# Six one-hots from one comparison with a scalar in a graph network kernel

## What is computed

```python
msg_input = jnp.concatenate([node_feats[src], edge_sh, edge_radial], axis=-1)
h = jax.nn.silu(msg_input @ W1 + b1)
h = jax.nn.silu(h @ W2 + b2)
messages = h @ W3 + b3
aggregated = jax.ops.segment_sum(messages, dst, num_segments=node_feats.shape[0])
```

## Time and profile before

| | |
|---|---|
| median of three timed runs | 4085.32 us |
| the profiled execution, its own time | 4067.74 us |
| its span | 4066.0 us |
| mean granted TensorE clock, share of full | 0.839 |
| PE busy (matmuls) | 3010.0 us, 74% |
| DVE busy | 1891.9 us, 47% |
| POOL busy | 1628.2 us, 40% |
| ACT busy | 1567.3 us, 39% |

### The profile page before, as it was taken

The page is one execution under the profiler, slowest core; times in us unless marked ns, Lnnn a source line. Parts: engine busy times, 40 slices in busy tenths (PEclk is TensorE's granted clock), DMA queues, the critical chain, the costliest instruction groups (busy, mean ns, idle before and its releaser), DMA issues.

```text
span 4066.0 us, 65736 instructions
## 1 busy us (share of the span) xinstructions
PE 3010.0 (74%) x21771; PEld 2333.6 (57%) x21771; DVE 1891.9 (47%) x2455; ACT 1567.3 (39%) x2617; POOL 1628.2 (40%) x1563
## 2 busy tenths in 40 slices
PE   3699997799963777776778777666777776677747
PEld 3477776798961455554555555554545555455546
DVE  5999998444550433333333333333334333333405
ACT  2688885233221333332333333333333333333415
POOL 3000000000006566665555666665554666656240
PEclk9999998899985888887878888887778888878866
DMA  2133333698971333333333333333333333333310
GB/s 101 80 156 144 158 144 156 256 366 326 360 248 31 90 89 85 87 86 76 86 84 88 89 86 87 86 84 80 80 79 85 88 86 87 85 80 89 87 22 16
DMA packets 204771, 477.12 MB, mean 117 GB/s; under 512 B 47656, under 2 KB 99034, under 8 KB 185709
## 3 DMA queue, kind: packets, MB, share of 16 engines
q1 hardware_dynamic: 153573, 422.33, 30.6%
q0 software_dynamic: 50144, 52.47, 7.5%
q10 hardware_dynamic: 1001, 1.66, 0.1%
HBM read 339.87 MB, written 136.41 MB: 117 GB/s over the span
## 4 chain that ended last, share of the span: by engine, by line
PE 53%; another core or an unknown queue 24%; issue 9%; DVE 9%; ACT 4%; DMA 1%; POOL 0%; DVEq 0%; ACTq 0%; POOLq 0%
PE ps L795 11%; PE ps L968 8%; PE ps L980 8%; PE ps L987 8%; PE ps L995 7%; PE ps L814 5%; PE ps L958 4%; DVE arena L1903 2%; DVE stageT L1879 1%; ACT ps L1351 1%; ACT arena L1346 1%; PE ps L1067 1%; PE ps L1044 0%; PE ps L846 0%
## 5 line engine op out<-in xcount | busy, mean ns | idle before, releaser
L663 POOL DMA_INDIRECT arena<-m_tab,m_idx x1463 | 1543.8, 1055 | 2207.5 <-issue 1574.7
L2150 DVE TENSOR_TENSOR_SCAN arena<-arena,ps 128x512 f32<-128x512 f32 x391 | 500.0, 1279 | 1294.4 <-ACT ps L1351 985.3
L995 PEld LDWEIGHTS ps<-weights,arena 128*128 128x128 f32 x3128 | 477.3, 219 | 537.8 <-issue 529.6
L995 PE MATMUL ps<-weights,arena 128*128 128x64 f32 x3128 | 468.3, 296 | 296.3 <-issue 229.0
L1346 ACT ACTIVATE arena<-ps,weights 128x512 f32<-128x512 f32 x391 | 268.4, 687 | 864.2 <-remote 390.6
L958 PE MATMUL ps<-ident,arena 128*64 128x128 f32 x1564 | 268.0, 298 | 383.0 <-DVE arena L2137 238.7
L980 PE MATMUL ps<-arena,weights 81*128 81x512 f32 x782 | 477.6, 692 | 71.0 <-issue 38.6
L795 PE MATMUL ps<-arena 128*128 128x195 bf16 (+1 forms) x4802 | 481.9, 248 | 32.2 <-DVE arena L1845 31.6
L968 PE MATMUL ps<-ends,arena 128*128 128x192 bf16 x4900 | 461.7, 250 | 29.3 <-issue 27.0
L987 PE MATMUL ps<-arena,weights 128*128 128x512 f32 x782 | 464.5, 676 | 13.7 <-issue 12.3
L795 PEld LDWEIGHTS ps<-arena 128*128 128x128 f16 x4802 | 417.1, 98 | 63.0 <-DVE arena L1845 31.7
(11 more groups left out here) (277 smaller groups left out, 2365.4 us busy)
## 6 DMA issues: line engine op xcount, KB each, us to landing
arena<-count_d SPq DMA_DIRECT2D x98, 1568.0 KB, 8.5
arena<-keep_d SPq DMA_DIRECT2D x391, 256.0 KB
count_d<-arena SPq DMA_DIRECT2D x49, 1568.0 KB, 5.1
scan_rows<-arena SPq DMA_DIRECT2D x391, 128.0 KB
arena<-m_tab,m_idx POOLq DMA_INDIRECT x1463
arena<-attr_in SPq DMA_DIRECT2D x391, 34.0 KB
arena<-src_row SPq DMA_DIRECT2D x25, 256.0 KB
wide<-hT_d SPq DMA_DIRECT2D x1, 1617.0 KB
```

Source lines behind the costliest of these rows:

```text
L663: pool.indirect_dma_start(m_rows[:, k, t, :], None, m_tab, bass.IndirectOffsetOnAxis(ap=m_idx[:, k, t:t + 1].bitcast(U32), axis=0))\
L995: last = pe.matmul(m_back[k % BACK_RING][:, t * D:(t + 1) * D], m_scan[:, k % SCAN_RING, t * P:(t + 1) * P], W("W3"), start=True, stop=True)
L2150: dve.tensor_tensor_scan(m_scan[:, k % SCAN_RING, :], m_mask[:, k % MASK_RING, :], m_term[k % TERM_RING], before, ALU.mult, ALU.add).then_ ...
```

## The change

The comparison with a table of numbers becomes a comparison with a scalar. At the beginning of a lap the source numbers are laid six times, the copy `a` less 128 a, in int16. Each group of six blocks is then one TENSOR_SCALAR that compares all six copies with one number a partition, `node_no[:, first]` = p + 128 first. The table `pick_no`, the small TENSOR_SCALAR of each group and two waits of each group go. The groups become eight of six blocks and one of one block. A copy has 516 numbers rather than 512, in three runs of 172; the six copies lie in three rows of 1032 numbers with a gap of two behind each, and the loaded numbers in three rows of 172 with a gap of two.

```diff
-PICKS = [(0, 6), (6, 6), (12, 6), (18, 6), (24, 5), (29, 5), (34, 5), (39, 5), (44, 5)]
+PICKS = [(a, min(6, J - a)) for a in range(0, J, 6)]
 PICK_RING, PICK_BLOCKS, PICK_LAG = 3, 6, 5
+PICK_RUNS, PICK_RUN = 3, 172
+PICK_COLS = PICK_RUNS * PICK_RUN
+PICK_PAIR = 2 * PICK_COLS
...
-        pick_int = carve(slots_at, BE).bitcast(I32)
-        pick_src, pick_from = (carve(slots_at + BE + n * BE // 2, BE // 2).bitcast(I16) for n in range(2))
-        pick_no = stage[:, :, :, :].rearrange("p s t f -> p (s t f)")[:, 0:PICK_BLOCKS * BE // 2].bitcast(I16)\
-            .rearrange("p (a e) -> p a e", a=PICK_BLOCKS)
+        pick_int = carve(slots_at, PICK_RUNS * (PICK_RUN + 2)).bitcast(I32)\
+            .rearrange("p (r e) -> p r e", r=PICK_RUNS)[:, :, 0:PICK_RUN]
+        pick_src = stage[:, :, :, :].rearrange("p s t f -> p (s t f)")[:, 0:PICK_BLOCKS // 2 * (PICK_PAIR + 2) // 2].bitcast(I16)\
+            .rearrange("p (r e) -> p r e", r=PICK_BLOCKS // 2)[:, :, 0:PICK_PAIR]
...
             def load_pick(lap):
-                sp.dma_start(pick_int, src_row[:, bass.ds((LOOP * lap + PICKED) * BE, BE)].partition_broadcast(P)).then_inc(pick_loaded, DMA)
+                sp.dma_start(pick_int, src_row[:, bass.ds((LOOP * lap + PICKED) * BE, PICK_COLS)].partition_broadcast(P)
+                             .rearrange("p o (r e) -> p (o r) e", r=PICK_RUNS)).then_inc(pick_loaded, DMA)
...
                 dve.wait_ge(pick_loaded, DMA * lap)
-                dve.tensor_copy(pick_src, pick_int).then_inc(pick_known, 1)
+                dve.wait_ge(pick_ready, len(PICKS) * (lap - 1) + 1)
+                for a in range(PICK_BLOCKS):
+                    last = dve.tensor_scalar(pick_src[:, a // 2, (a % 2) * PICK_COLS:(a % 2 + 1) * PICK_COLS]
+                                             .rearrange("p (r e) -> p r e", r=PICK_RUNS), pick_int, float(-P * a), None, ALU.add)
+                last.then_inc(pick_known, 1)
+                dve.wait_ge(pick_known, lap)
...
             def mark_pick(lap, n):
 
                 first, blocks = PICKS[n]
-                dve.wait_ge(pick_known, (1 + len(PICKS)) * (lap - 1) + n + 1)
-                dve.wait_ge(pick_ready, len(PICKS) * (lap - 1) + n + 1)
-                dve.tensor_scalar(pick_from, pick_src, float(-P * first), None, ALU.add).then_inc(pick_known, 1)
-                dve.wait_ge(pick_known, (1 + len(PICKS)) * (lap - 1) + n + 2)
                 dve.wait_ge(pick_used, len(PICKS) * (lap - 1) + n + 1)
-                dve.tensor_tensor(pick[:, n % PICK_RING, 0:blocks, :], pick_from.unsqueeze(1).to_broadcast([P, blocks, BE]),
-                                  pick_no[:, 0:blocks, :], ALU.is_equal).then_inc(pick_ready, 1)
+                of = pick[:, n % PICK_RING, 0:blocks * PICK_COLS]
+                if blocks == PICK_BLOCKS:
+                    of, src = of.rearrange("p (r e) -> p r e", r=PICK_BLOCKS // 2), pick_src
+                else:
+                    src = pick_src[:, 0, 0:blocks * PICK_COLS]
+                dve.tensor_scalar(of, src, node_no[:, first:first + 1], None, ALU.is_equal).then_inc(pick_ready, 1)
...
-                    link(dve.tensor_copy(pick_no, per_node(node_no[:, 0:PICK_BLOCKS], BE)))
```

More of the change, by code:

```diff
@@ L200, in build @@
         slots_at += OUT_RING * TB * D
-        pick = carve(slots_at, PICK_RING * PICK_BLOCKS * BE // 2).bitcast(BF16).rearrange("p (k a e) -> p k a e", k=PICK_RING, a=PICK_BLOCKS)
-        slots_at += PICK_RING * PICK_BLOCKS * BE // 2
-        pick_int = carve(slots_at, BE).bitcast(I32)
-        pick_src, pick_from = (carve(slots_at + BE + n * BE // 2, BE // 2).bitcast(I16) for n in range(2))
-        pick_no = stage[:, :, :, :].rearrange("p s t f -> p (s t f)")[:, 0:PICK_BLOCKS * BE // 2].bitcast(I16)\
-            .rearrange("p (a e) -> p a e", a=PICK_BLOCKS)
+        pick = carve(slots_at, PICK_RING * PICK_BLOCKS * PICK_COLS // 2).bitcast(BF16)\
+            .rearrange("p (k c) -> p k c", k=PICK_RING)
+        slots_at += PICK_RING * PICK_BLOCKS * PICK_COLS // 2
+        pick_int = carve(slots_at, PICK_RUNS * (PICK_RUN + 2)).bitcast(I32)\
+            .rearrange("p (r e) -> p r e", r=PICK_RUNS)[:, :, 0:PICK_RUN]
+        pick_src = stage[:, :, :, :].rearrange("p s t f -> p (s t f)")[:, 0:PICK_BLOCKS // 2 * (PICK_PAIR + 2) // 2].bitcast(I16)\
+            .rearrange("p (r e) -> p r e", r=PICK_BLOCKS // 2)[:, :, 0:PICK_PAIR]
         node_parts = ends[:, :, :].rearrange("p j f -> p (j f)")[:, 0:J * PARTS * D // 2].bitcast(BF16)\
@@ L569, in _ @@
                     move_slot(LOOP * i + k, k)
-                sp.wait_ge(pick_known, (1 + len(PICKS)) * (i - 1) + 1)
+                sp.wait_ge(pick_known, i)
                 load_pick(i + 1)
@@ L968, in pick_rows @@
                         last = pe.matmul(ps[:, 3 + TERM_RING + t // 2, (t % 2) * PARTS * D:(t % 2 + 1) * PARTS * D],
-                                         pick[:, n % PICK_RING, a - first, t * P:(t + 1) * P],
+                                         pick[:, n % PICK_RING, (a - first) * PICK_COLS + t * P:(a - first) * PICK_COLS + (t + 1) * P],
                                          node_parts[:, a, :, :].rearrange("p q d -> p (q d)"),
```

## The result

| | kernel before | changed kernel |
|---|---|---|
| median, us (4 runs each, one chip) | 4090.5 | 4514.94 |
| from, to | 4084.05, 4100.86 | 4501.55, 4526.65 |
| ratio, 95% interval | | 1.1034 [1.0992, 1.1076] |
| profiled execution, its span | 4067.74, 4066.0 | 4501.55, 4499.8 |

It is 10.3% slower; 4500 was forecast.

What follows compares the result with a forecast made beforehand. It took laps to be bounded by PE's work plus freezes during POOL's unheld gathers: 117.9 us a lap against 100.5, times 24, adds 418 to 4067.7, and with 17.6 gives 4500 us; its own range was 4390 to 4600.

Steps and rivals of the forecast that it cites:

- The compare: Lap stage, DVE: each 3096-element compare takes 1.76 us and does not hold POOL's gathers.
- Rival A: Lap stage: the compare runs short, 0.94 us, and part of the hold on gathers stays; 4265 us, chance 0.12.
- Rival B: Lap stage: the compare takes 1.76 us and holds gathers as the old one does; 4085 to 4111 us, chance 0.10.
- Hidden beside PE: Lap stage: DVE's marks, 14.4 us a lap, stand beside PE's picks and cost nothing.
- The source numbers: Lap start, DVE: six casts take 2.4 to 4.1 us instead of 0.4; 0 to 1.2 us a lap come through.
- The inference on which the prediction hung: Lap stage: the other engines freeze after some 8 us of unheld POOL gathers, and held gathers prevent it.
- The lap of 3003: Kernel before: a lap whose marks held few gathers froze at 26 us and took 112.5 us.
- Rival C: Freeze tied to place in the program or burst length, not unheld gathers; 154 us less, 3931 us, chance 0.15.
- an onset of 10 us: Pick-stage bursts: freeze allowed to begin at 10 us, not 8, as small DVE operations may hold a gather; 117.9 us a lap.
- three bursts of 25, 25 and 20 us: POOL's gathers per lap after the change: the 40 split in two, since the second 20's indices need PE.
- 4.1 us of recovery: Lap stage: time at half clock after each freeze, 4.1 us, for two freezes a lap before and three after.
- A lap = PE's 61.2 + frozen time ...: Lap stage: a lap is PE's 61.2 us, plus frozen time less what PE does in it, plus recovery at half clock.

Runs made afterwards that it cites:

- two_runs: The changed kernel with the source numbers in two spaced runs of 1548 instead of three of 1032: 3275.46 us, 0.9631 of the kernel before.
- tensor_tensor_again: The changed kernel with its eight long compares made by tensor_tensor again, layout, casts and grouping kept: 4133.86 us, 1.0136 of the kernel before.
- fewer_gathers: The changed kernel with 52 instead of 56 gathers a lap, output not the reference's: 3066.35 us, 0.9007 of the kernel before.
- chip 5: The changed kernel run unaltered on a chip where the kernel before took 3406.99 us: 3184.24 us, 0.9347 of it.
- paced form: The changed kernel with GpSimd waiting for the scan ahead of each slot's four gathers but the first of five: 3176.51 us, 0.9354 of the kernel before.
- the pacing of the old kernel: The kernel before with GpSimd waiting for the scan ahead of each slot's four gathers but the first of five: 3983.29 us, beside 4179.38 unaltered.

## Why the prediction was right, and where it was not

*The compare.* 1.80 us against 1.76, and no hold: right. Of the two reasons given, the one read from the rows doesn't stand: "it is cut differently on both sides" is as true of two_runs, two runs against one, which takes 1.017 us and holds. The one on the counts, three against 3096 and neither both even nor equal, agrees with both runs. The 1.76 was the row of another operation; that it came within 0.04 is in part luck. Rival A (short, partial hold) is what two_runs is. Rival B needed the hold to stay; it is gone.

*Hidden beside PE.* Right: leaving the compares out gave 3180 against 3184 us. That was measured where nothing freezes; with the freeze it wasn't tried.

*The source numbers.* 0.678 us a cast, 4.1 a lap, the upper end. What of it came through I can't separate: the table's residue is under 20 us either way.

*The inference on which the prediction hung*, that held gathers prevent the freeze: tensor_tensor_again, on a chip that freezes, shows that the operation which holds them keeps the freeze off; that the holding does it remains an inference. The lap of 3003 was misread: six of its gathers were held, not few, and its freeze began during one. "8 us after the last held gather" fits the usual laps and is no rule. Rival C, the freeze tied to the place in the program, is refuted by the changed kernel's own windows: it now comes 8 us into the burst that had been clean for 41.

*The sum.* Lap starts of PE-released bursts, 1390.32 and 24 laps later 4250.73 in the changed kernel:

```profile
1390.32 0.94 POOL L668 DMA_INDIRECT arena<-m_tab,m_idx  x1 [14.54 <-PE ps L963]
...
4250.73 0.94 POOL L668 DMA_INDIRECT arena<-m_tab,m_idx  x1 [14.38 <-PE ps L963]
```

119.2 us a lap, where 117.9 was taken with an onset of 10 us and 121.3 with 8 everywhere. The onset was about 8 (the allowance of 2 us for small operations was wrong; one hold of 0.13 us in 56 gathers), and PE got a little more done in the freezes than 0.15 (6.62 x 0.58 / 17 = 0.23 in the first). The two errors cancel in part. 433.8 us between the profiled runs are 18.1 a lap; 17.4 were forecast. The prediction's three bursts of 25, 25 and 20 us came out as such. The 4.1 us of recovery for each freeze was what was left over in one lap of the kernel before, and no run shows it by itself; that the sum came within 1% with it owes something to luck.

*What was wrong*, though it didn't touch the time on that chip: "A lap = PE's 61.2 + frozen time ...". PE's 61.2 is nearly right as PE's work (62.6 a lap at a clock of 0.99 in fewer_gathers), but it is not what a lap comes down to without the freeze. That is GpSimd's 56 x 1.25 = 70.0 us (and 8.5 of held gathers in the kernel before), which stood in the earlier trace rows as the start-to-start of two gathers; I used that pitch for the bursts and never multiplied it by 56. It was masked since PE's frozen time left GpSimd waiting. From there I wrote "If nothing else moved, the big burst would end 6.4 us earlier" as a side remark, where held gathers, 8.5 us of them a lap, are nearly the whole gain on a chip without the freeze (204 of 223 us). And I took the freeze for a property of the program. The traces shown could not tell it from one of the chip; a forecast for another chip by my sum would have been wrong in sign.

## What to carry to other kernels

Multiply the fixed start-to-start of an engine's repeated operation by its count per lap before calling it off the critical path; here that number names the bound wherever the rest is undisturbed. Lengthening an operation can pay if the longer form leaves another engine alone: 1.80 us that hold no gather beat 1.02 us that do, by 91 us over 24 laps. And when engines with work at hand stand still together, take the same unaltered kernel to a second chip before reasoning on: this change was 10% slower in the first measurement and 6.5% faster on chip 5.

## What the runs showed of the hardware

- On some chips all engines but GpSimd nearly stop while it gathers without a break: PE does 13 to 20 matmuls in 13 to 17 us and its granted clock falls to 0.56 to 0.62. In bursts without held gathers it begins 6 to 8 us in and lasts until the burst is over or nearly so. It was there in the first measurement and on two of the six chips, and not on four, with the same gathers at 0.945 us. What differs between them is open: nothing in these traces shows it, and no chip was met twice, so it may be the moment and not the chip.
- A tensor_tensor of two 16-bit operands (1.05 to 1.76 us) holds a gather beside it to 1.8 to 2.2 us. The Trainium skill (SBUF — State Buffer, Who interferes with whom) infers that a tensor_tensor, taking only the read side of the shared pair, doesn't hold up descriptor generation; the rows of tensor_tensor_again (2.04 to 2.20 us beside it, 0.94 otherwise) show that it does hold these gathers. They also read their indices, `m_idx`, from SBUF, and the same section says that an instruction with two SBUF inputs contends with a GpSimd instruction that reads SBUF; which of the two is at work no run tells apart.
- A tensor_scalar of int16 to bf16 with 3096 elements takes 1.800 us from three runs and leaves 1120 gathers at a mean of 946 ns; from two runs it takes 1.017 us and the gathers' mean is 1019.
- An indirect DMA of 128 rows keeps GpSimd busy for 0.945 us, and the next begins 1.25 us after it: 56 of them set a lap of 70.0 us, 52 one of 65.0.

The changed kernel and its paced form (3184 and 3177 us, the same within their spread) are the fastest complete ones where nothing freezes. No kernel was shown to beat the kernel before on every chip: on one that freezes only the pacing of the old kernel, in a single run, came out under it, and the paced form of the changed kernel wasn't run there.
